# Splitting the transpose evacuations of a transformer layer between VectorE and ScalarE, and reordering its LoRA stage

## The reference

```python
x = x + attn(layernorm(x), Wq, Wk, Wv, Wo)      # RoPE on q and k, causal softmax
t = layernorm(x)
logits = t @ Wr.T                                # 4 experts
gates  = softmax(keep only the top 2 of logits)
mid    = einsum('tf,erf->ter', t, A)             # 4 x 16 numbers a token
x = x + sum_e gates[e] * (mid[e] @ B[e]) * 4.0
```

## Time and profile before

| | us |
|---|---|
| median of the 2 runs shown | 4300.34 |
| the 2 runs | 4220.12 and 4380.56 |
| the profiled execution | 4233.71 |
| span of its slowest core (core 1) | 4232.1 |
| spans of the 8 cores | 4202.3 to 4232.1 |

### The profile page before, as it was taken

One profiled execution on the slowest core, in us unless ns is written; L12 is line 12 of the kernel. 1 busy time (PEld: TensorE's weight loads), 2 busy tenths in 40 slices (PEclk: granted clock), 3 DMA queues, 4 the chain that ended last, 5 costly groups with the idle time before them and its releaser, 6 DMA issues.

```text
span 4232.1 us, 46081 instructions; the slowest of 8 cores (4202.3 to 4232.1 us)
## 1 busy us (share of the span) xinstructions
PE 3238.3 (77%) x17520; PEld 1517.4 (36%) x17520; DVE 1159.5 (27%) x2589; ACT 900.7 (21%) x917; POOL 72.5 (2%) x86
## 2 busy tenths in 40 slices
PE   4676766767438998789439998879737999887994
PEld 2222323222213444434214444434313444443441
DVE  4111117000353223400461222220253221212016
ACT  2000004000111004600220007810011003983001
POOL 0000000000000000000000000000000000000000
PEclk9888887888758999899659999989857999998995
DMA  7999991999434551044044540024233552002431
GB/s 166 184 197 177 204 184 35 195 172 188 81 142 146 167 170 67 21 159 151 29 179 155 176 167 16 1 110 150 99 119 135 178 170 85 1 1 80 151 128 80
DMA packets 215704, 530.63 MB, mean 125 GB/s; under 512 B 82112, under 2 KB 168256, under 8 KB 169408
## 3 DMA queue, kind: packets, MB, share of 16 engines
q1 hardware_dynamic: 53280, 421.72, 27.6%
q0 software_dynamic: 87456, 84.97, 15.0%
q10 hardware_dynamic: 74752, 20.99, 2.4%
HBM read 474.19 MB, written 117.44 MB: 140 GB/s over the span
## 4 chain that ended last, share of the span: by engine, by line
PE 57%; DMA 17%; DVE 11%; ACT 9%; issue 4%; DVEq 0%; ACTq 0%; SPq 0%; POOLq 0%
PE pd L293 47%; ACT epair L577 8%; DMA wblk<-wo 5%; DMA wblk<-wq 5%; DVE bst L333 4%; PE pd L612 4%; PE pd L319 3%; PE pd L553 3%; DMA wscr<-wblk 2%; DMA h<-x 1%; DMA wblk<-wv 1%; DVE epair L589 1%; DMA wblk<-wk 1%; DVE hnT L303 1%; DVE aoT L303 1%
## 5 line engine op out<-in xcount | busy, mean ns | idle before, releaser
L293 PE MATMUL pd<-xnT,wblk 128*128 128x512 bf16 x5120 | 1164.0, 391 | 136.8 <-DMA wblk<-wq 109.6
L293 PE MATMUL pd<-wblk,aoT 128*128 128x512 bf16 x4096 | 934.6, 392 | 146.9 <-DMA wblk<-wo 109.9
L293 PEld LDWEIGHTS pd<-xnT,wblk 128*128 128x128 bf16 x5120 | 510.7, 100 | 789.3 <-issue 226.6
L577 ACT ACTIVATE epair<-pd,cvals 128x1024 bf16<-128x1024 f32 x544 | 629.6, 1201 | 319.6 <-PE pd L553 276.6
L293 PEld LDWEIGHTS pd<-wblk,aoT 128*128 128x128 bf16 x4096 | 409.8, 100 | 670.9 <-issue 221.1
L612 PE MATMUL pd<-vaug,epair 128*128 128x129 bf16 x4352 | 356.4, 222 | 162.9 <-ACT epair L577 95.5
L319 PE MATMUL pd<-iden,xnhn 128*128 128x128 bf16 x1024 | 144.4, 301 | 392.3 <-ACT xnhn L349 351.4
L612 PEld LDWEIGHTS pd<-vaug,epair 128*128 128x128 bf16 x4352 | 265.9, 98 | 415.5 <-issue 410.0
L366 DVE TENSOR_TENSOR t1b<-qswp,sing 128x512 bf16<-128x512 bf16 x160 | 110.8, 692 | 1059.1 <-DMA qswp<-qt 887.4
L695 DVE TENSOR_TENSOR h<-pd,h 128x512 f32<-128x512 f32 x128 | 79.5, 683 | 1006.7 <-PE pd L293 1006.7
L337 ACT ACTIVATE lnv<-agg,cvals 128x1 f32<-128x1 f32 x32 | 9.4, 294 | 1574.7 <-DVE agg L335 1574.7
(11 more groups left out here) (55 smaller groups left out, 918.0 us busy)
## 6 DMA issues: line engine op xcount, KB each, us to landing
wblk<-wscr SPq DMA_DIRECT2D x240, 1024.0 KB, 5.4
wscr<-wblk SPq DMA_DIRECT2D x80, 1024.0 KB, 8.0
h<-x SPq DMA_DIRECT2D x24, 2048.0 KB, 9.8
wblk<-wq POOLq DMA_DIRECT2D x32, 1024.0 KB, 14.4
wblk<-wo POOLq DMA_DIRECT2D x32, 1024.0 KB, 14.1
out<-h SPq DMA_DIRECT2D x16, 2048.0 KB, 6.7
qswp<-qt ACTq DMA_DIRECT2D x256, 64.0 KB, 5.4
wblk<-wk POOLq DMA_DIRECT2D x8, 1024.0 KB, 13.0
```

Source lines behind the costliest of these rows:

```text
L293: nc.tensor.matmul(o, l, r, start=st, stop=sp))
L577: nc.scalar.activation(epair[p][:, 0:ncols], src, AF.Exp, bias=cvals[:, 3:4], scale=cvals[:, 2:3]))
```

## The change

Four edits:

1. `evac_quad` takes an engine. `transpose_tile` gives the quads with even cq to VectorE as before and those with odd cq to ScalarE, as an Identity activation. The lists of evacuations that later matmuls wait for hold both engines' values.
2. Stage E goes through its tiles in the order 2, 3, 0, 1 (`E_ORDER`), in the layer norm and in what follows.
3. The one copy into `midlog_sb` and the one into `gmidT` are done tile by tile, 68 and 128 columns each.
4. The loop over the gates and the loop over the additions and outputs become one: a tile's gate chain, its two matmuls (bank 4 or 7 in turn), its `gmidT` copy, its eight additions and its output, and only then the next tile's gate chain.

The numbers of instructions on TensorE and the bytes moved stay as they were.

```diff
-    def evac_quad(bank, dstT, cq, jl, extra_waits):
+    def evac_quad(bank, dstT, cq, jl, extra_waits, eng="V"):
...
+        if eng == "V":
+            vv = sch.V([("T", bank.writer)] + extra_waits,
+                       lambda e, d=dst, s=src: nc.vector.tensor_copy(d, s))
+            rd = ("V", vv)
+        else:
+            vv = sch.A([("T", bank.writer)] + extra_waits,
+                       lambda e, d=dst, s=src: nc.scalar.activation(
+                           d, s, AF.Identity))
+            rd = ("A", vv)
+        bank.readers.append(rd)
+        return rd
...
-            ew = first_evac_waits if cq == 0 else []
-            res.append((cq, evac_quad(bank, dstT, cq, jl, ew)))
+            ew = first_evac_waits if cq <= 1 else []
+            res.append((cq, evac_quad(bank, dstT, cq, jl, ew,
+                                      "V" if cq % 2 == 0 else "A")))
...
-                           waits=[wv, ("V", xnT_blk_ready[b])])
+                           waits=[wv] + xnT_blk_ready[b])
...
+        E_ORDER = [2, 3, 0, 1] if c.GT == 4 else list(range(c.GT))
+        hnT_blk_ready = [[] for _ in range(nblk)]
         wq0 = rg_qtar.take(("hnT", g))
-        for jl in range(c.GT):
+        for pos, jl in enumerate(E_ORDER):
...
-        vml = sch.V([("T", bank_t.writer)] + msb_users[0],
-                    lambda e: nc.vector.tensor_copy(
-            midlog_sb[:, 0:c.GT * c.EW], bank_t.ap[:, 0:c.GT * c.EW]))
-        msb_users[0] = []
-        bank_t.readers.append(("V", vml))
-
-        bank_gt = psum[4]
-        for jl in range(c.GT):
+
+        for pos, jl in enumerate(E_ORDER):
+            vml = sch.V([("T", bank_t.writer), ("V", gate_last[0])] + msb_users[0],
+                        lambda e, jl=jl: nc.vector.tensor_copy(
+                            midlog_sb[:, jl * c.EW:(jl + 1) * c.EW],
+                            bank_t.ap[:, jl * c.EW:(jl + 1) * c.EW]))
+            msb_users[0] = []
+            bank_t.readers.append(("V", vml))
...
+            gate_last[0] = vgm
+            msb_users[0].append(("V", vgm))
+            msb_users[0].append(("A", aex))
+            bank_gt = psum[4] if pos % 2 == 0 else psum[7]
+            w = [("V", vgm), iden_ready] + bank_gt.readers
+            bank_gt.readers = []
...
-        wgt = rg_gmidT.take(("gt", g))
-        vgt = sch.V([("T", bank_gt.writer)] + wgt, lambda e: nc.vector.tensor_copy(
-            gmidT[:, 0:c.GT * 128], bank_gt.ap[:, 0:c.GT * 128]))
-        bank_gt.readers.append(("V", vgt))
-
-        for jl in range(c.GT):
+            wgt = rg_gmidT.take(("gt", g, jl))
+            vgt = sch.V([("T", bank_gt.writer)] + wgt,
+                        lambda e, b=bank_gt, jl=jl: nc.vector.tensor_copy(
+                            gmidT[:, jl * 128:(jl + 1) * 128], b.ap[:, 0:128]))
+            bank_gt.readers.append(("V", vgt))
+
             last_add = 0
             for sl in range(c.D // 512):
                 bank = psum[5 + sl % 2]
```

More of the change, by code:

```diff
@@ L410, in build_program @@
         nblk = (c.NCH + 7) // 8
-        xnT_blk_ready = [0] * nblk
+        xnT_blk_ready = [[] for _ in range(nblk)]
         axv = [0] * c.GT
@@ L428, in build_program @@
                                          warena):
-                if jl == c.GT - 1 and (cq % 2 == 1 or cq == c.NCH // 4 - 1):
-                    xnT_blk_ready[min(cq // 2, nblk - 1)] = vv
+                if jl == c.GT - 1:
+                    xnT_blk_ready[min(cq // 2, nblk - 1)].append(vv)
             rg_xnhn.use("T", sch.cnt["T"])
         for b in range(nblk):
-            if xnT_blk_ready[b] == 0:
+            if not xnT_blk_ready[b]:
                 xnT_blk_ready[b] = xnT_blk_ready[-1]
@@ L649, in build_program @@
         rg_qtar.use("T", sch.cnt["T"])
-        aoT_blk_ready = [0] * nblk
+        aoT_blk_ready = [[] for _ in range(nblk)]
         wq0 = rg_qtar.take(("aoT", g))
@@ L657, in build_program @@
                     wq0 if jl == 0 else []):
-                if jl == c.GT - 1 and (cq % 2 == 1 or cq == c.NCH // 4 - 1):
-                    aoT_blk_ready[min(cq // 2, nblk - 1)] = vv
+                if jl == c.GT - 1:
+                    aoT_blk_ready[min(cq // 2, nblk - 1)].append(vv)
             rg_hs[jl // 2].use("T", sch.cnt["T"])
         for b in range(nblk):
-            if aoT_blk_ready[b] == 0:
+            if not aoT_blk_ready[b]:
                 aoT_blk_ready[b] = aoT_blk_ready[-1]
@@ L688, in build_program @@
                            start=(ci == 0), stop=(ci == c.NCH - 1),
-                           waits=[wv, ("V", aoT_blk_ready[b])])
+                           waits=[wv] + aoT_blk_ready[b])
                 rg_wblk[buf].use("T", sch.cnt["T"])
@@ L711, in build_program @@
                                          lambda ci, a3s=a3s: [("A", a3s[ci // 8])],
-                                         wq0 if jl == 0 else []):
-                if jl == c.GT - 1 and (cq % 2 == 1 or cq == c.NCH // 4 - 1):
-                    hnT_blk_ready[min(cq // 2, nblk - 1)] = vv
+                                         wq0 if pos == 0 else []):
+                if pos == c.GT - 1:
+                    hnT_blk_ready[min(cq // 2, nblk - 1)].append(vv)
             rg_xnhn.use("T", sch.cnt["T"])
         for b in range(nblk):
-            if hnT_blk_ready[b] == 0:
+            if not hnT_blk_ready[b]:
                 hnT_blk_ready[b] = hnT_blk_ready[-1]
@@ L723, in build_program @@
                start=(ci == 0), stop=(ci == c.NCH - 1),
-               waits=[awr_ready, ("V", hnT_blk_ready[ci // 8])])
+               waits=[awr_ready] + hnT_blk_ready[ci // 8])
         rg_qtar.use("T", sch.cnt["T"])
@@ L730, in build_program @@
         bank_t = psum[3]
-        for jl in range(c.GT):
-            w = [("A", aml), iden_ready] + (bank_t.readers if jl == 0 else [])
-            if jl == 0:
+        for pos, jl in enumerate(E_ORDER):
+            w = [("A", aml), iden_ready] + (bank_t.readers if pos == 0 else [])
+            if pos == 0:
                 bank_t.readers = []
@@ L786, in build_program @@
                                 g4v[:, e4:e4 + 1], 0.0, OP.mult, OP.add))
[L787 to L791, removed]
+            gate_last[0] = vgm
[4 more added lines that the diff above has]
+            bank_gt.readers = []
+            sch.T(w, lambda e, b=bank_gt: nc.tensor.matmul(
+                b.ap[0:c.NE * c.R, 0:128],
                 gmid[:, :], iden[:, :], start=True, stop=True))
-            tv = sch.T([], lambda e, jl=jl: nc.tensor.matmul(
-                bank_gt.ap[c.NE * c.R:2 * c.NE * c.R, jl * 128:(jl + 1) * 128],
+            tv = sch.T([], lambda e, b=bank_gt: nc.tensor.matmul(
+                b.ap[c.NE * c.R:2 * c.NE * c.R, 0:128],
                 gmid[:, :], iden[:, :], start=True, stop=True))
```

7 lines of the change are left out of this document (1 added, 6 removed).

## The result

The change makes the kernel slower. The ratio of the changed kernel to the one before is 1.0108, with a 95% interval of 1.0065 to 1.015, or about 46 us of 4235. The medians of all executions are 4298.67 us (12) against 4239.91 us (10).

What follows compares the result with a forecast made beforehand. The prediction took the touched stages to be bound by chains of handovers between engines, not an engine's throughput. Its terms, 34 + 0 + 22 + 0 = +56 us on the profiled 4233.7, gave 4290 us, range 4245 to 4360.

Steps and rivals of the forecast that it cites:

- within 2%: Whole kernel: time between 4149 and 4318 us, taken as indistinguishable from no change; chance 0.86, slower 0.12, faster 0.02.
- my own bounds: Whole kernel: all terms at their low or high ends give +35 to +91 us, so 4269 to 4325.
- Edit 1, stages A and E: Layer-norm tiles: odd quads' evacuations queue behind ScalarE's normalising activations; 4.3 us lost a stage, 34 us in eight stages.
- the handover from ScalarE to TensorE: Layer-norm transposes: time from ScalarE's evacuation to the next matmul, taken as 0.24 us.
- my lower bound: Layer-norm stages: with a handover of 0.14 us the split costs 27 us in all.
- Edit 1, stage D: Stage D's transposes: bank 0's own 1.53 us loop stays with VectorE, so 0 us, bounds -2 to +6.
- The rival that splitting shortens the transposes: Stage D and layer-norm tiles: a second evacuating engine saves 38 and 48 us, giving 4170 us; chance 0.07.
- Edits 3 and 4: Stage E's gates and additions: four round trips replace one, 11.85 us a tile, 5.6 us a group, +22 in all.
- Edit 2: Group boundaries: the x load still queues behind the outputs, so the new tile order gives 0 us, bounds -8 to +12.
- Rival 1: Stage D and layer-norm tiles: splitting evacuations between two engines shortens the transposes, giving 4170 us; chance 0.07.
- Rival 2: Group boundaries: the x load hides behind stage E's last tiles, three 16 us waits gone, 4242 us; chance 0.05.
- rival 4: Group boundaries: three transfers share equally and take 20.1 us, giving 4302 us; counted within the main case's 0.76.
- Rival 3: All split transposes: ScalarE's evacuation is dearer in place; 0.3 us more a loop gives 4338 us; chance 0.10.

Runs made afterwards that it cites:

- e2_split_only: Odd transpose quads evacuated by ScalarE in all stages, nothing else, on the kernel before; ratio 1.0058 (1.0034 to 1.0082).
- e7_interleaved: Kernel before with the split in all stages, quad 1's and 3's evacuations queued between ScalarE's normalising activations; three executions, 4211.5 to 4229.5 us.
- e10_changed_four_banks: The changed kernel with its transposes turning through four PSUM banks instead of two; ratio 0.9863 (0.9838 to 0.9887) against the kernel before.
- e4_split_in_D: The kernel before with evacuations split between VectorE and ScalarE in stage D only; ratio 1.0007 (0.9981 to 1.0033).
- e3_order: The kernel before with only stage E's tile order changed to 2, 3, 0, 1; ratio 0.9994 (0.9967 to 1.0022).
- e5_loads_early: The changed kernel with the next group's first two x loads issued between the outputs; three executions at 4225.0, 4225.1 and 4235.1 us.

## Why the prediction was right and wrong

**The sum and its parts held; what I made of the sum did not.** The forecast was 4290 us, +56 on the profiled execution, or +1.3%. The profiled execution came out at 4279.85, +46, and the ratio says +1.08%. The median of all executions, 4298.67 us, lies inside the range of 4245 to 4360, but that it lies so near 4290 is luck: the sum was made on the profiled execution. But I gave "within 2%" a chance of 0.86, on the sentence that about 2% is what a measurement of this kernel can tell from no change. That step failed. The interval came out at 0.4% to either side, so a sum of 1.3% is a forecast of slower, and slower by 1.08% is what the runs showed. I should have named it as the direction; my own bounds, 4269 to 4325, did not reach the kernel before.

**Edit 1, stages A and E: mechanism right, the 34 us too large by 10.** Predicted 4.3 us a stage, measured 3 x 0.55 + 1.44 = 3.1 in stage E. Stage A with what follows it scatters more: three of them are 13.9 us longer on core 1 and 8.6 on core 4. e2_split_only gives 24 us in all. The mis-sized term is the handover from ScalarE to TensorE. I took 0.24 us, from L349 to the first matmul; behind the odd evacuations it is 0.14 (1144.77 + 0.57 to 1145.48), the value of my lower bound, 27 us. The first evacuation also began at 4.54 and not 4.63: it overlaps the activation before it by 0.1 us. e7_interleaved and e10_changed_four_banks show the two halves of the mechanism apart: the queue and the bank.

**Edit 1, stage D: right.** 0 us in my bounds of -2 to +6; measured -1.1 to the last evacuation of either engine (-1.3 in e4_split_in_D). The rival that splitting shortens the transposes stands refuted for two banks. With four banks and both engines it is true: 54 us in stage D. The advice of the Trainium skill, page "TensorEngine Tiling (Array Packing)", section "PSUM Bottleneck", to use both engines for evacuation, holds in this kernel only once each engine has a second bank to work on while its first is refilled: with both engines 32 quads take about 23.8 us on two banks and 10.7 on four.

**Edits 3 and 4: mechanism right, somewhat large.** Predicted 5.6 us a group and 22 in all, measured 4.8 and 19.1. The 68-column copy took 0.22 (predicted 0.23). The 128-column copy took 0.29 (L641's 0.35 taken). A tile took 11.53 us and not 11.85. Of the 0.32 us, 0.06 is that copy and 0.11 the gates with their handover (4.19 from 1189.28 to 1193.47, predicted 4.30). The other 0.15 is the additions: their pace is 0.763 us here (six in 4.58) where I had averaged in the one stall in the earlier trace rows, and the next tile's copy starts 0.08 us before the last addition ends.

**Edit 2: right.** The wait for x stayed: 46.4 us at three boundaries against 48.2. e3_order and e5_loads_early show that the order alone gives nothing and that the queue's order was the cause. The Trainium skill, page "DMA: Bandwidth & Descriptors", section "Two DMAs through the same engine are not ordered", says that within one queue of one DMA engine descriptors start in order but are pipelined. The traces agree roughly: with three transfers issued right behind one another they land 9.2, 15.3 and 20.6 us after issue. For the first load that lies between the 13.4 of strict turns and the 20.1 of equal shares.

**The rivals.** Rival 1 is answered under stage D. Rival 2 did not happen (46.4 us of waits), nor did rival 4 (15.3 us and not 20.1). Rival 3, a dearer evacuation on ScalarE, did not happen either: 0.591 to 0.597 us in its place, L457's value.

## What to carry to other kernels

Work that is moved to an idle engine enters that engine's queue where the program puts it: look at what stands ahead of it there, and at which bank or buffer it holds while it waits. Where two buffers are handed back and forth in a loop of waits, a second engine changes next to nothing until each engine has two buffers of its own. A buffer freed earlier helps only if the transfer into it is issued earlier, and a transfer put ahead of another delays that one: look at who waits for it. And a small loss that a sum gives with bounds on one side of zero is a forecast, not "no change".

## What the runs showed of the hardware

With two banks TensorE's granted clock in stage D's transposes is 0.50; with four banks it is 1.00. Windows of e10_changed_four_banks (core 7, 709 to 718 us) and of the changed kernel (core 0, the start of the stage and then 733 to 752 us); the columns are length, busy time of the five engines, clock, DMA share and GB/s:

```profile
709.00:718.00 9.00, 8.30 (x112) 6.46 (x112) 8.73 (x14) 7.49 (x13) 0.00 (x0) 1.00 0.45 158
```

```profile
728.50:731.80 3.30, 1.28 (x20) 0.96 (x17) 2.15 (x8) 0.60 (x1) 0.00 (x0) 1.00 0.02 5
...
733.00:752.00 19.00, 12.59 (x101) 9.47 (x98) 8.82 (x13) 7.27 (x13) 0.00 (x0) 0.50 0.31 111
```

Both begin the stage at a granted clock of 1.00 (2.4 GHz). In the changed kernel TensorE then stood idle for 1.94, 0.72 and, from there on, 0.52 us before each pair of quads, and from 733 us on the granted clock is 0.50 (1.2 GHz). With four banks it stood idle once, for 1.50 us, then ran 112 matmuls without a gap, and the clock stayed. The lower clock makes the bank's loop longer: two quads' eight matmuls take 0.61 us at 1.00 (at 731.12) and 1.01 at 0.50 (at 733.98), and a pair 1.33 us and 1.53. Four banks brought 13.4 us a group and not the 9 that I had worked out from the slow clock; that the clock is all of that difference was not tested by itself.
